# A layer with a long convolution, cross attention and a quantized feed-forward part: context and weights laid out on the host, context products from SBUF

## Chip, cores and metric

The kernel runs on one core of a Trainium2 chip. The metric is the device time of one execution in microseconds, lower is better. Engines are named as in the profile: PE is TensorE, PEld its weight loads, DVE is VectorE, ACT is ScalarE, POOL is GpSimd, and SP is the queue of SyncE, which issues all the DMAs.

## What is computed

A decoder layer with three parts, each with a residual and a layer norm: a Hyena convolution, a cross attention that is a convolution too, and a feed-forward part with weights rounded to -1, 0 and 1.

```python
x = _layernorm(x + hyena(x, ...))                       # (16, 256, 512)
# cross attention, k = v = ctx_2048, q = x, heads of 8 rows
kv = jnp.einsum('bhil,bhjl->bijhl', k_, v_)             # products of the context with itself
y = irfft(rfft(kv, 2 * L) * rfft(ssm_kernel, 2 * L))[..., :L]
out = jnp.einsum('bijhl,bhil->bjhl', y + kv * D, q_)
x = _layernorm(x + out)
# feed-forward: w1 (2048, 512), w2 (512, 2048)
w_quant = clip(round(w * rms), -1, 1) / rms
x_quant = clip(round(x * scale), -128, 127) / scale
h = gelu(x_quant @ w1_quant.T); out = quantized(h) @ w2_quant.T
x = _layernorm(x + out)
```

There are 32 heads of 8 rows, and 16 x 512 positions. As k and v are the same context, only 36 products of pairs are made for each position instead of 64.

## The kernel before

The program has two blocks. `hyena_block` does the first part for two halves of the batch and, toward its end, gets the rounded weights of the feed-forward part ready. `heads_block` then does cross attention and feed-forward head by head: one head is 16 x 8 = 128 rows of 512.

**The end of the first block.** In its last stretch the output projection is done in 16 blocks (`out_part` on TensorE, L554; `res_stat` and `res_norm` on VectorE). The residual has four buffers: SP loads block R + 3 when the result of block R - 1 has been stored (`load_res`, `store_res`). Between the blocks the eight parts of w1 and w2 are rounded: SP loads a part of 1 MB (`load_part`), ScalarE scales and rounds it (`round_part`), VectorE clips it (`clip_part`), TensorE turns 16 squares of 128x128 through PSUM (`turn_part`, L608), and ScalarE writes them as f16 from PSUM, half a part at a time (`copy_part`, L768). The context of the first head is turned here as well (`turn_first_ctx`), and its products are made after block 12 (`first_pairs`).

**The loop over heads.** Every engine has a `body(n)` with its instructions in a fixed order; step n works on several heads at once. For a head the context goes this way: SP loads 128 rows of 512 (`load_ctx`, 256 KB), ScalarE reverses each block of 128 (`reverse_blocks`, L1166), TensorE turns the four blocks into `ctx_bank` in PSUM (`turn_ctx`, L1395), ScalarE copies them to SBUF with each group of 8 written twice (`copy_twice` into `kx`, L1171), and VectorE makes the 36 products (`far_pairs`, L1183, 4 of them; `near_pairs`, L1177, 32 of them) with one operand from `ctx_bank` and the other from `kx`. `sum_blocks` (L1674) adds two blocks of products into `kv_sum`, both operands in SBUF.

The products then go through TensorE as a Toeplitz matrix product (L1412) into `conv_bank`, in four blocks `tb`. VectorE multiplies each with the query (`times_q_up`, `times_q_dn`, writing `z`), reading `conv_bank` in PSUM and `qx` in SBUF. GpSimd sums `z` in `add_up`, four instructions (L1830, L1832, L1835, L1839), the last of which writes `att`. `z` has two buffers, so VectorE's block `tb` waits for the `att` of block `tb` - 2. `att` is turned (`turn_back`), added to the residual and normalized, rounded, and goes through the feed-forward part one to four steps later.

The orders that matter are, on GpSimd in step n: `add_up` of the last block of head n-1; `rstd_of_out`, which waits for `o_mv`; `add_up` block 0 of head n; `rstd_of_att`; `add_up` blocks 1 and 2. On VectorE: last half of `z` of head n-1, scale of g, `z` block 0 (it waits for the `att` of block 2 of head n-1), `far_pairs` and `near_pairs` of head n+1, `o_mv` (`mean_of_out`), the output sum, the residual sum, `z` block 1, and so on, with `kv_sum` near the end.

Of the kernel before, what the change touches and what calls it, by code (L numbers as in the profile page):

```python
# [13 lines left out]
P = 128  # L14
# [4 lines left out]
F = 2048  # L19
# [33 lines left out]
def hyena_block(nc, w, early, dram):  # L53
# [24 lines left out]
    with ExitStack() as ctx:  # L78
# [130 lines left out]
        part_turned = sem("part_turned")  # L209
# [12 lines left out]
        PART_AT = {1 + i: i for i in range(2 * PARTS)}  # L222
        CTX_AT, PAIRS_AT = 11, 12
# [49 lines left out]
        with nc.Block() as block:  # L273
            @block.sync
            def _(sp):
# [50 lines left out]
                def part_source(i):  # L326
                    if i < PARTS:
                        return dram["w1"].rearrange("(q n p) d -> p q n d", p=P, q=PARTS)[:, i, :, :]
                    return dram["w2"][(i - PARTS) * P:(i - PARTS + 1) * P, :]

                def part_target(i, tile):
                    return tile.rearrange("p (n d) -> p n d", d=D) if i < PARTS else tile
# [82 lines left out]
                for hf in range(HALF):  # L415
                    if hf + 1 == HALF:
# [34 lines left out]
                    for t in range(T):  # L451
# [8 lines left out]
                        if hf + 1 == HALF and t == CTX_AT + 1:  # L460
                            sp.wait_ge(early["ctx_reversed"], 1)
                            sp.dma_start(early["ctx_tok"][:, 0, :], dram["ctx"][:, 2 * HD:3 * HD, :]).then_inc(early["ctx_loaded"][0], 16)

            @block.tensor
            def _(pe):
# [131 lines left out]
                def turn_part(i):  # L597
                    pe.wait_ge(clipped, i + 1)
                    low = view(part_raw[i].bitcast(F16), 0, (2, F))
                    for hh in range(2):  # L600
                        if i >= 2:
                            pe.wait_ge(part_done, 2 * (i - 2) + hh + 1)
                        elif hh == 0:
                            pe.wait_ge(ch_copied, 4 * HALF * DC)
                        out = turn_bank[2 * (i % 2) + hh][:, :, :].rearrange("p a b -> p (a b)").bitcast(F16)
                        for j in range(FC // 2):
                            fc = hh * FC // 2 + j
                            last = nc.tensor.transpose(out[:, j * P:(j + 1) * P], low[:, fc * P:(fc + 1) * P], w["ident16"][:, :])  # L608
                        last.then_inc(part_turned, 1)

# [577 lines left out]
def heads_block(nc, w, early, dram):  # L1188
# [6 lines left out]
    with ExitStack() as ctx:  # L1195
# [119 lines left out]
        with nc.Block() as block:  # L1315
            @block.sync
            def _(sp):
# [647 lines left out]
```

## Time and profile before

| | |
|---|---|
| median of three runs | 1036.88 us (1036.31 to 1039.31) |
| span of the profiled execution | 1030.8 us |
| busy: PE, PEld | 977.3 us (95%), 582.6 us (57%) |
| busy: DVE, ACT, POOL | 813.1, 617.1, 569.0 us (79%, 60%, 55%) |
| moved by DMA | 148.89 MB |

A busy share is an average over the whole span. GpSimd's 55% is made of a first half in which it has little to do and a second half in which it is busy nine tenths of the time, so the two halves are to be read apart. The first block ends near 457 us. The profiled execution's own time isn't given; its span is 6.1 us below the median.

### The profile page before, as it was taken

What the parts mean: (1) busy time and instruction counts of PE and PEld (TensorE: products, weight loads), DVE (VectorE), ACT (ScalarE), POOL (GpSimd) and SP (SyncE); (2) the same over time, 40 slices, a digit from 0 to 9 for tenths busy, and PEclk for the clock granted to TensorE, in tenths of its full rate; (3) what the DMA queues carried; (4) which work ended last, traced back from release to release, by engine and by line L of the source; (5) the groups of instructions that cost most, each with busy time, mean ns of one, the idle gap of its engine ahead of it and who ended that gap; (6) DMA issues with size and microseconds to landing.
All of it is one profiled execution on the core that took longest, in us unless ns stands there. A gap on an engine that the chain in (4) does not pass through costs nothing.

```text
span 1030.8 us, 14820 instructions
## 1 busy us (share of the span) xinstructions
PE 977.3 (95%) x4555; PEld 582.6 (57%) x4555; DVE 813.1 (79%) x1539; ACT 617.1 (60%) x759; POOL 569.0 (55%) x890
## 2 busy tenths in 40 slices
PE   3899999999999999988999999999999999999985
PEld 2455555544455554546666666666666666666641
DVE  6977985786554656666999898989889898989872
ACT  5755544202565657413676767777777777777674
POOL 5410410132000002439989888989898989898861
PEclk9999999999999999989999999999999999999997
DMA  9323655365576679453454646464646464544333
GB/s 320 77 62 123 183 169 168 117 197 172 165 251 208 204 245 310 146 166 86 86 129 106 144 105 146 103 148 99 150 101 149 103 141 110 134 114 111 77 73 81
DMA packets 186924, 148.89 MB, mean 144 GB/s; under 512 B 100501, under 2 KB 141497, under 8 KB 184825
## 3 DMA queue, kind: packets, MB, share of 16 engines
q1 hardware_dynamic: 186872, 148.26, 53.2%
q8 instruction: 26, 0.43, 0.2%
q14 instruction: 26, 0.20, 0.1%
HBM read 93.49 MB, written 33.77 MB: 123 GB/s over the span
## 4 chain that ended last, share of the span: by engine, by line
POOL 36%; DVE 7%; issue 5%; PE 5%; ACT 1%; POOLq 1%; DMA 0%; DVEq 0%; ACTq 0%
POOL sum L1830 15%; POOL sum L1832 8%; POOL att L1839 4%; POOL sum L1835 3%; PE conv_bank L1412 3%; DVE kv L1177 2%; POOL a_rstd L1849 1%; DVE block_diag L1177 1%; POOL o_rstd L1860 1%; DVE z L1700 1%; PE hq_bank L1481 1%; PE back_bank L1500 1%; POOL a_shift L1851 1%; POOL a_rstd L1846 1%; POOL o_shift L1862 1%
## 5 line engine op out<-in xcount | busy, mean ns | idle before, releaser
L1830 POOL TENSOR_TENSOR sum<-z 128x640 f32<-128x640 f32 x128 | 204.9, 1601 | 3.1 <-DVE z L1703 3.1
L845 DVE SCALAR_TENSOR_TENSOR conv_all<-u,taps,conv_all 128x1024 f32<-128x1024 f32 x92 | 122.4, 1331 | 91.3 <-ACT conv_all L716 89.4
L1412 PE MATMUL conv_bank<-block_diag 128*128 128x288 f32 x508 | 140.0, 416 | 3.6 <-ACT conv_bank L1569 1.9
L1412 PE MATMUL conv_bank<-kv,block_diag 128*128 128x288 f32 x512 | 137.5, 407 | 2.6 <-ACT conv_bank L1569 1.5
L1481 PE MATMUL hq_bank<-x_lo,hq_t 128*128 128x512 f16 x512 | 123.2, 386 | 4.0 <-DMA hq_t<-hq_int 4.0
L1691 DVE TENSOR_TENSOR z<-conv_bank,qx 128x512 f32<-128x512 f32 x128 | 88.0, 687 | 43.4 <-POOL att L1839 29.7
L708 ACT ACTIVATE u<-slot_bank,bias,unscale 128x1024 f32<-128x1024 f32 x46 | 55.4, 1205 | 108.5 <-PE slot_bank L517 82.5
L1832 POOL TENSOR_TENSOR sum<-sum 128x320 f32<-128x320 f32 x128 | 112.4, 878 | 10.0
L1412 PEld LDWEIGHTS conv_bank<-block_diag 128*128 128x128 f32 x508 | 96.7, 196 | 31.0 <-ACT conv_bank L1569 2.4
L554 PE MATMUL slot_bank<-wout_t,y 128*128 128x512 f32 x256 | 112.8, 594 | 0.0
L1412 PEld LDWEIGHTS conv_bank<-kv,block_diag 128*128 128x128 f32 x512 | 94.1, 190 | 29.3 <-DVE z L1703 2.6
L517 PE MATMUL slot_bank<-x_lo,w_hi 128*128 128x512 f16 x384 | 91.1, 379 | 3.3 <-DVE x_lo L833 3.3
L1055 POOL TENSOR_SCALAR r_rstd<-r_meanvar 128x1 f32<-128x1 f32 x32 | 19.7, 615 | 133.3 <-DVE r_meanvar L869 133.3
L517 PE MATMUL slot_bank<-x_hi,w_hi 128*128 128x512 f16 x384 | 91.1, 379 | 1.7 <-ACT x_hi L688 0.8
L517 PE MATMUL slot_bank<-x_hi,w_lo 128*128 128x512 f16 x384 | 91.0, 379 | 0.0
L1754 DVE TENSOR_REDUCE g_max<-g 128x1 f32<-128x512 f32 x128 | 86.3, 676 | 5.2 <-ACT g L1617 5.2
L1481 PEld LDWEIGHTS hq_bank<-x_lo,hq_t 128*128 128x128 f16 x512 | 50.7, 99 | 64.6 <-DMA hq_t<-hq_int 4.5
L554 PEld LDWEIGHTS slot_bank<-wout_t,y 128*128 128x128 f32 x256 | 47.6, 190 | 54.3 <-issue 53.8
L1617 ACT ACTIVATE g<-back_bank,x_unscale 128x512 f32<-128x512 f32 x64 | 43.8, 684 | 57.6 <-PE back_bank L1500 57.6
L1578 ACT ACTIVATE hq_f<-g,h_scale 128x1024 f32<-128x1024 f32 x64 | 73.5, 1148 | 5.8 <-DVE h_scale L1749 5.8
L1839 POOL TENSOR_TENSOR att<-sum 128x128 f32<-128x128 f32 x128 | 65.2, 510 | 10.4 <-POOL sum L1835 0.8
L1700 DVE TENSOR_TENSOR z<-conv_bank,qx 128x384 f32<-128x384 f32 x128 | 69.3, 541 | 0.0
(187 smaller groups left out, 1775.8 us busy)
## 6 DMA issues: line engine op xcount, KB each, us to landing
x_quad<-in_w SPq DMA_DIRECT2D x10, 1024.0 KB, 8.0
v_scratch<-conv_all SPq DMA_DIRECT2D x16, 512.0 KB, 3.3
c_scratch<-v_tok SPq DMA_DIRECT2D x8, 1024.0 KB, 5.3
y<-c_scratch SPq DMA_DIRECT2D x8, 1024.0 KB, 4.9
res<-in_x SPq DMA_DIRECT2D x32, 256.0 KB, 3.0
x_scratch<-res SPq DMA_DIRECT2D x32, 256.0 KB, 3.2
block_diag<-in_ctx SPq DMA_DIRECT2D x32, 256.0 KB, 5.0
block_diag<-ssm_scratch SPq DMA_DIRECT2D x32, 256.0 KB, 4.0
```

The costliest lines, as they stand in the source:

```text
L517: last = nc.tensor.matmul(slot_bank[n % 2][:, q, :], wt[:, dc, e * P:(e + 1) * P], xt[:, dc, cols], start=(j == 0 and dc == 0), stop=(j == ...
L554: last = nc.tensor.matmul(slot_bank[R // 2 % 2][:, R % 2, :], y[:, cc, t, :], w["wout_t"][:, cc, :], start=(cc == 0), stop=(cc == DC - 1))
L845: ins = nc.vector.scalar_tensor_tensor(out=acc, in0=(u_first[kind] if n < 3 else u)[:, t0 + tap:t0 + tap + T // 2, :].rearrange("p t b -> ...
L1412: last = nc.tensor.matmul(view(conv_bank[tb % 2][:, hh, :], 0, (ROW64, T // 2), (1, PAIRS)), toep[:, head.buf, window * P:(window + 1) * P ...
L1481: last = nc.tensor.matmul(hq_bank[:, :], hq_t[:, fc, :], w["w2_t"][:, fc, :], start=(fc == 0), stop=(fc == FC - 1))
L1578: nc.scalar.activation(hq_f[:, half], g[:, half], ACT.Copy, scale=h_scale[:, 0:1], bias=LOW_HALF).then_inc(hq_rounded, 1)
L1691: nc.vector.tensor_tensor(view(z[:, b, :, :], 0, (4 * PLANE, T), (PLANE + 1, 4), (1, HD)), view(conv, 0, (ROW64, T), (HD, 4), (1, HD)), vi ...
L1700: nc.vector.tensor_tensor(view(z[:, b, :, :], DN, (4 * PLANE, T), (PLANE, 3), (1, HD)), view(conv, HD, (ROW64, T), (HD, 3), (1, HD)), view ...
L1754: nc.vector.tensor_reduce(g_max[:, k:k + 1], g[:, k * 512:(k + 1) * 512], AX_X, ALU.max, apply_absolute_value=True).then_inc(g_maxed, 1)
L1830: nc.gpsimd.tensor_tensor(sum2[:, :, :], z[:, b, :, 0:half], z[:, b, :, half:2 * half], ALU.add).then_inc(sum2_done, 1)
L1832: nc.gpsimd.tensor_tensor(sum1[:, :, :], sum2[:, :, 0:PLANE], sum2[:, :, PLANE:half], ALU.add).then_inc(sum1_done, 1)
L1839: nc.gpsimd.tensor_tensor(att[:, head.buf, tb, :].rearrange("p (t j) -> p t j", j=HD), sum1[:, :, DN:PLANE], sum1[:, :, 0:HD], ALU.add).th ...
```

## The change

- The host hands over the context already turned and reversed, with each group of 8 written twice (`ctx_turned`, 32 x 128 x 1024), and w1 and w2 transposed. `load_ctx`, `reverse_blocks`, `turn_ctx`, `copy_ctx` and `ctx_bank` go; `load_kx` loads 512 KB a head straight into `kx`, which has two buffers now.
- `near_pairs` and `far_pairs` read both operands from `kx`.
- `turn_part` and `copy_part` go; `narrow_part` writes a whole part as f16 from SBUF. `turn_first_ctx` goes, and `first_pairs` comes after block 9.
- The f16 identity isn't made. The initial loads of parts are w1 in rows of 2048 and w2 in four pieces of 512.

```diff
-        PART_AT = {1 + i: i for i in range(2 * PARTS)}
-        CTX_AT, PAIRS_AT = 11, 12
+        PAIRS_AT = 9
...
-                            sp.dma_start(early["ctx_tok"][:, h, :], dram["ctx"][:, heads, :]).then_inc(early["ctx_loaded"][h], 16)
+                            sp.dma_start(early["kx"][:, h, :], dram["ctx_turned"][h]).then_inc(early["kx_loaded"][h], 16)
...
+                def narrow_part(i):
+                    act.wait_ge(clipped, i + 1)
+                    if i == 0:
+                        act.wait_ge(slot_full, HALF * NSLOT)
+                    out = (x_hi, x_lo)[i // PARTS][:, i % PARTS, :]
+                    nc.scalar.activation(out, view(part_raw[i].bitcast(F16), 0, (2, F)), ACT.Copy, bias=-HALF_ONE).then_inc(part_done, 1)
...
-def near_pairs(nc, k, kx, kv):
+def near_pairs(nc, kx, kv):
 
     W2 = 2 * HD
-    return nc.vector.tensor_tensor(view(kv, 0, (PAIRS, LB * T), (HD, 4), (1, HD)), view(k, 0, (HD, LB * T), (0, 4), (1, HD)),
+    return nc.vector.tensor_tensor(view(kv, 0, (PAIRS, LB * T), (HD, 4), (1, HD)), view(kx, 0, (W2, LB * T), (0, 4), (1, HD)),
                                    view(kx, 0, (W2, LB * T), (1, 4), (1, HD)), ALU.mult)
...
-def far_pairs(nc, k, kx, kv):
-
-    return nc.vector.tensor_tensor(view(kv, 4 * HD, (PAIRS, LB * T), (1, 4)), view(k, 0, (HD, LB * T), (1, 4)),
+def far_pairs(nc, kx, kv):
+
+    return nc.vector.tensor_tensor(view(kv, 4 * HD, (PAIRS, LB * T), (1, 4)), view(kx, 0, (2 * HD, LB * T), (1, 4)),
                                    view(kx, 4, (2 * HD, LB * T), (1, 4)), ALU.mult)
...
+                def load_kx(head):
+                    sp.wait_ge(kv_done, head.back(2).count(1, 1))
+                    sp.dma_start(kx[:, head.buf, :], dram["ctx_turned"][head.c]).then_inc(kx_loaded[head.buf], 16)
...
                 def body(n):
                     h1, h3 = n.back(1), n.back(3)
-                    if n.c == 0:
-                        load_ctx(n.back(-3))
+                    if n.c >= 1 and n.back(-2).exists():
+                        load_kx(n.back(-2))
...
-                    if n.back(-4).exists():
-                        load_ctx(n.back(-4))
```

In the instruction order this shows at three places. First SP's queue in one step of the loop over heads, before (`in_ctx` is the context, `x_scratch` the first part's result, `ssm_scratch` the Toeplitz rows):

```order
L1354 DMA_TRANSPOSE xq_t<-xq_int 128x4x128 [waits xq_packed]
L1320 DMA block_diag<-x_scratch 128x1x512 [waits x1_turned]
L1320 DMA x_res<-x_scratch 128x1x512 [waits a_steps]
L1335 DMA block_diag<-ssm_scratch 128x512 [waits conv_full]
L1336 DMA block_diag<-ssm_scratch 128x2x128
L1320 DMA block_diag<-in_ctx 128x1x512 [waits ctx_reversed]
L1358 DMA_TRANSPOSE hq_t<-hq_int 128x8x128 [waits hq_packed] x2
```

And after:

```order
L1306 DMA_TRANSPOSE xq_t<-xq_int 128x4x128 [waits xq_packed]
L1277 DMA block_diag<-in_ctx_turned 128x1024 [waits kv_done]
L1273 DMA block_diag<-x_scratch 128x1x512 [waits x1_turned]
L1273 DMA x_res<-x_scratch 128x1x512 [waits a_steps]
L1287 DMA block_diag<-ssm_scratch 128x512 [waits conv_full]
L1288 DMA block_diag<-ssm_scratch 128x2x128
L1310 DMA_TRANSPOSE hq_t<-hq_int 128x8x128 [waits hq_packed] x2
```

The context's load moved from behind the other loads of the step to before them and is twice as large.

Second TensorE at the end of a step, before (`z_done` frees a bank of the convolution):

```order
L1412 MATMUL conv_bank<-block_diag 128x8x36 x6
L1407 MATMUL back_bank<-ident,block_diag 128x128 [waits g_done,x1_loaded1]
L1407 MATMUL back_bank<-ident,block_diag 128x128 x3
L1395 MATMUL ctx_bank<-ident,block_diag 128x128 [waits kv_done,ctx_reversed]
L1395 MATMUL ctx_bank<-ident,block_diag 128x128 x3
L1412 MATMUL conv_bank<-kv,block_diag 128x8x36 [waits z_done,kv_done,toep_loaded1]
```

And after:

```order
L1441 MATMUL back_bank<-x_hi,xq_t 128x512 [waits g_done]
L1441 MATMUL back_bank<-x_hi,xq_t 128x512 x3
L1353 MATMUL conv_bank<-block_diag 128x8x36 x6
L1348 MATMUL back_bank<-ident,block_diag 128x128 [waits g_done,x1_loaded1]
L1348 MATMUL back_bank<-ident,block_diag 128x128 x3
L1353 MATMUL conv_bank<-kv,block_diag 128x8x36 [waits z_done,kv_done,toep_loaded1]
```

The four transposes of the context are gone, and nothing else moved.

Third VectorE at the products in a step, before (`z` is the product with the query, `o_mv` the mean and variance of the output):

```order
L1691 TENSOR_TENSOR z<-conv_bank,qx 128x16x4x8 [waits att_done]
L1700 TENSOR_TENSOR z<-conv_bank,qx 128x16x3x8
L1703 TENSOR_TENSOR z<-conv_bank,qx 128x16x8
L1660 REGISTER_ALU
L1662 REGISTER_ALU [waits kx_done]
L1183 TENSOR_TENSOR block_diag<-ctx_bank,block_diag 128x64x4 [waits conv_full]
```

And after, with the large product and `o_mv`, which follow in both:

```order
L1611 TENSOR_TENSOR z<-conv_bank,qx 128x16x4x8 [waits att_done]
L1620 TENSOR_TENSOR z<-conv_bank,qx 128x16x3x8
L1623 TENSOR_TENSOR z<-conv_bank,qx 128x16x8
L1581 ISA
L1583 REGISTER_ALU [waits kx_loaded0]
L1138 TENSOR_TENSOR block_diag<-block_diag 128x64x4 [waits conv_full]
L1704 ISA
L1706 REGISTER_ALU [waits o_steps]
L1132 TENSOR_TENSOR block_diag<-block_diag 128x64x32 [waits o_shifted]
L1690 BN_AGGR o_mv<-o_stats 128x2
```

The place is the same; the operand from `ctx_bank` has become one from `block_diag`, the SBUF tile in which `kx` lies, and the wait is for the load instead of ScalarE's copy.

## Rows read from the trace of the kernel before

**Rows 1.** Timeline of GpSimd (POOL): start us, duration us, instruction [idle before it].

```profile
539.51 0.19 POOL L1857 TENSOR_TENSOR o_rstd<-o_mv,eps_col 128x1 f32<-128x1 f32 x1 [1.26 <-DVE o_mv L1770]
...
963.36 0.19 POOL L1857 TENSOR_TENSOR o_rstd<-o_mv,eps_col 128x1 f32<-128x1 f32 x1 [0.82 <-DVE o_mv L1770]
```

**Rows 2.** Waits between 500 and 1000 us: total, times, longest.

```profile
DVE z L1691 <- POOL att L1839: 26.9, 26, 1.3
...
POOL o_rstd L1857 <- DVE o_mv L1770: 21.6, 26, 1.3
```

**Rows 3.** Timeline of VectorE (DVE), one step of the loop over heads.

```profile
705.15 0.69 DVE L1691 TENSOR_TENSOR z<-conv_bank,qx 128x512 f32<-128x512 f32 x1 [1.22 <-POOL att L1839]
...
706.42 0.41 DVE L1183 TENSOR_TENSOR block_diag<-ctx_bank,block_diag 128x256 f32<-128x256 f32 x1
706.75 2.28 DVE L1177 TENSOR_TENSOR block_diag<-ctx_bank,block_diag 128x2048 f32<-128x2048 f32 x1
708.95 0.17 DVE L1770 BATCH_NORM_AGGREGATE o_mv<-o_stats 128x2 f32<-128x6 f32 x1
...
717.70 0.98 DVE L1674 TENSOR_TENSOR kv_sum<-block_diag 128x576 f32<-128x576 f32 x1
...
722.08 0.69 DVE L1691 TENSOR_TENSOR z<-conv_bank,qx 128x512 f32<-128x512 f32 x1 [0.90 <-POOL att L1839]
```

**Rows 4.** Timeline of GpSimd in the same step.

```profile
704.97 1.55 POOL L1830 TENSOR_TENSOR sum<-z 128x640 f32<-128x640 f32 x1
706.60 0.87 POOL L1832 TENSOR_TENSOR sum<-sum 128x320 f32<-128x320 f32 x1
...
707.92 0.45 POOL L1839 TENSOR_TENSOR att<-sum 128x128 f32<-128x128 f32 x1
709.20 0.19 POOL L1857 TENSOR_TENSOR o_rstd<-o_mv,eps_col 128x1 f32<-128x1 f32 x1 [0.82 <-DVE o_mv L1770]
...
718.02 2.07 POOL L1830 TENSOR_TENSOR sum<-z 128x640 f32<-128x640 f32 x1
```

**Rows 5.** Timeline of TensorE (PE): two turns of the context; an earlier idle time.

```profile
702.16 0.60 PE L1395 MATMUL ctx_bank<-ident,block_diag 128*128 128x128 f32 x4
702.60 1.14 PE L1412 MATMUL conv_bank<-kv,block_diag 128*128 128x288 f32 x4
...
719.11 0.60 PE L1395 MATMUL ctx_bank<-ident,block_diag 128*128 128x128 f32 x4
...
489.41 1.24 PE L1412 MATMUL conv_bank<-block_diag 128*128 128x288 f32 x4 [1.93 <-ACT conv_bank L1569]
```

**Rows 6.** Groups of ScalarE (ACT) instructions: count, busy us, mean ns, idle before.

```profile
L1171 ACT COPY block_diag<-ctx_bank 128x1024 f32<-128x1024 f32 x31 | 31.5, 1017 | 0.0
...
L1166 ACT COPY block_diag<-block_diag 128x512 f32<-128x512 f32 x32 | 19.5, 612 | 1.3 <-DMA block_diag<-in_ctx 1.3
```

**Rows 7.** Timelines of VectorE and GpSimd where `kv_sum` meets GpSimd's instructions.

```profile
513.96 2.09 DVE L1674 TENSOR_TENSOR kv_sum<-block_diag 128x576 f32<-128x576 f32 x1
...
515.52 1.27 POOL L1832 TENSOR_TENSOR sum<-sum 128x320 f32<-128x320 f32 x1
...
734.50 0.75 DVE L1674 TENSOR_TENSOR kv_sum<-kv 128x576 f32<-128x576 f32 x1
...
734.56 1.00 POOL L1839 TENSOR_TENSOR att<-sum 128x128 f32<-128x128 f32 x1
```

**Rows 8.** Timelines of TensorE and VectorE near the end of the first half.

```profile
421.12 1.06 PE L608 MATMUL conv_bank<-ident,u 128*128 128x128 f16 x16
...
431.18 0.69 DVE L865 TENSOR_TENSOR res<-slot_bank,res 128x512 f32<-128x512 f32 x1 [1.55 <-DMA res<-in_x]
```

**Rows 9.** Stretches: busy PE, PEld, DVE, ACT, POOL; granted clock, DMA share, GB/s.

```profile
400.00:410.00 10.00, 9.64 (x52) 4.83 (x50) 5.21 (x9) 10.00 (x9) 3.98 (x4) 1.00 1.05 312
490.00:495.00 5.00, 5.00 (x17) 3.52 (x16) 4.39 (x8) 1.35 (x2) 4.46 (x9) 0.66 0.17 52
1000.00:1005.00 5.00, 3.47 (x17) 1.41 (x16) 3.86 (x13) 4.44 (x6) 1.02 (x4) 1.00 0.12 26
```

More of the change, by code:

```diff
@@ L595, in sum_matrix @@
                     nc.tensor.matmul(turn_bank[0][:, 0, 0:2], ones[:, :], total[:, :], start=True, stop=True).then_inc(summed, 1)
[L597 to L609, printed above, removed]
-                def turn_first_ctx():
-                    pe.wait_ge(early["ctx_reversed"], 1)
-                    pe.wait_ge(part_done, 2 * (2 * PARTS - 2) + 1)
-                    for lb in range(LB):
-                        last = nc.tensor.transpose(turn_bank[0][:, lb, :], early["ctx_rev"][:, 0, lb * P:(lb + 1) * P], w["ident"][:, :])
-                    last.then_inc(early["ctx_turned"], 1)
                 def convolve_first(tb):
@@ L1320, in load @@
                     return lambda: sp.dma_start(tile[:, head.buf, :], src).then_inc(loaded[head.buf], 16)
-                def load_ctx(head):
-                    start = load("ctx", ctx_tok, head, ctx_loaded)
-                    sp.wait_ge(ctx_reversed, head.back(2).count(1, 1))
-                    start()
+                def load_kx(head):
+                    sp.wait_ge(kv_done, head.back(2).count(1, 1))
+                    sp.dma_start(kx[:, head.buf, :], dram["ctx_turned"][head.c]).then_inc(kx_loaded[head.buf], 16)
                 def load_x1(head):
@@ L1388, in _ @@
             def _(pe):
-                def turn_ctx(head):
-                    pe.wait_ge(ctx_reversed, head.count(1, 1))
-                    if head.c >= 1:
-                        pe.wait_ge(kv_done, head.back(1).count(1, 1))
-                    for lb in range(LB):
-                        last = nc.tensor.transpose(ctx_bank[:, lb * P:(lb + 1) * P], ctx_rev[:, head.buf, lb * P:(lb + 1) * P], w["ident"][:, :])
-                    last.then_inc(ctx_turned, 1)
                 def turn_x1(head):
@@ L1935, with laid_out @@
 _INPUTS = {
-    "x": "x", "ctx_2048": "ctx", "L0_attn_ln_gamma": "ln_gamma", "L0_attn_ln_beta": "ln_beta", "L0_attn_W_in": "W_in",
+    "x": "x", "L0_attn_ln_gamma": "ln_gamma", "L0_attn_ln_beta": "ln_beta", "L0_attn_W_in": "W_in",
     "L0_attn_b_in": "b_in", "L0_attn_short_w": "short_w", "L0_attn_short_b": "short_b", "L0_attn_k": "k",
     "L0_attn_conv_bias": "conv_bias", "L0_attn_W_out": "W_out", "L0_xattn_ssm_kernel": "ssm_kernel",
-    "L0_xattn_D": "ssm_D", "L0_ffn_w1": "w1", "L0_ffn_w2": "w2",
+    "L0_xattn_D": "ssm_D",
 }
+def laid_out(inputs, np):
+    once = np.asarray(inputs["ctx_2048"]).reshape(T, H, HD, LB, P)[..., ::-1].transpose(1, 4, 3, 0, 2)
+    twice = np.stack([once, once], axis=4)
+    return {
+        "ctx_turned": np.ascontiguousarray(twice).reshape(H, P, LB * T * 2 * HD),
+        "w1_t": np.ascontiguousarray(np.asarray(inputs["L0_ffn_w1"]).T),
+        "w2_t": np.ascontiguousarray(np.asarray(inputs["L0_ffn_w2"]).T),
+    }
 def kernel(**inputs):
@@ L1955 @@
         dram[short] = nc.dram_tensor(f"in_{short}", a.shape, _mybir.dt.from_np(a.dtype), kind="ExternalInput").ap()
+    for short, a in laid_out(inputs, _np).items():
+        arrays[f"in_{short}"] = a
+        dram[short] = nc.dram_tensor(f"in_{short}", a.shape, _mybir.dt.from_np(a.dtype), kind="ExternalInput").ap()
     dram["out"] = nc.dram_tensor("out_0", (T, B, D), F32, kind="ExternalOutput").ap()
```

91 lines of the change are left out of this document (21 added, 70 removed).

## The prediction, made before the changed kernel ran

> **What bounds the kernel now.** I read the waits first, then the timelines of three engines over one step of the loop over heads, because that loop fills the second half of the run. Its steps are alike: GpSimd's first instruction of the output variance starts 26 times, at 539.51 first and at 963.36 last, so 25 steps take 16.95 us each [rows 1]. Over the same stretch VectorE waits 26 times for GpSimd's `att`, and GpSimd 26 times for VectorE's `o_mv` [rows 2]: the two wait for each other, once a step each.
>
> The ring can be followed in one step. VectorE starts `z` at 705.15, when GpSimd has finished an `att`; then come the small and the large product of the context (706.42 and 706.75) and `o_mv` at 708.95 [rows 3]. GpSimd meanwhile does one `add_up` from 704.97 on, is done before `o_mv` is there, idles 0.82 us, and starts the rest of its step at 709.20 [rows 4]. From there to the next `z` at 722.08 [rows 3] are 12.88 us of GpSimd work without a pause. So the ring is 4.05 us (705.15 to 709.20) plus 12.88 us, 16.93 us in all, and it has no slack except those 0.82 us, on GpSimd's side of its first part.
>
> TensorE is as full: from one transpose of the context to the next, 702.16 to 719.11, are 16.95 us, and its groups follow each other with no idle time [rows 5]. Two rings of equal length lie side by side. A saving on one of them alone is worth nothing, and a cost on one is paid at once.
>
> **What the change takes away in the loop.** TensorE loses four transposes a head, 702.16 to 702.60 or 0.44 us [rows 5]: its ring would be 16.51 us. ScalarE loses the copy with both halves (1017 ns) and the reversal (612 ns) [rows 6]; ScalarE is on neither ring, so this I cost at nothing, the cover being GpSimd's work. If TensorE alone set the pace, 31 heads would give 31 x 0.44 = 13.6 us. Since the other ring stands at 16.93 us, the gain is nothing: what is late next is `att`, as now.
>
> **What it adds in the loop.** The products have the same shapes, 128x256 and 128x2048, but both operands now come from SBUF. The trace has one such VectorE instruction in the loop, `kv_sum`, 576 elements. It and GpSimd's instructions exclude each other. At 717.70 it takes 0.98 us, against 0.75 us when it finds the way free [rows 3, 7], and GpSimd's `sum` at 718.02 takes 2.07 us [rows 4], against 1.55 us at 704.97: GpSimd lost 0.52 us. At 734.50 it is first and takes 0.75 us, and GpSimd's `att` beside it takes 1.00 us, where another takes 0.45 (707.92) [rows 4, 7]: lost 0.55 us. At 513.96 it comes just after a long GpSimd instruction has begun, takes 2.09 us, and the next GpSimd instruction takes 1.27 us [rows 7] where 0.87 is usual (706.60) [rows 4]: lost 0.40 us, and VectorE lost 1.34. The products with one operand from PSUM do no such thing: the large one runs from 706.75 to 709.03 across GpSimd's instruction at 706.60, which keeps its 0.87 us.
>
> So I price the lock at 0.52 us for 576 elements, 0.90 ns an element: 2304 elements make 2.08 us. The engine's own pace is higher: from 256 elements to 2048 the instruction grows from 0.41 to 2.28 us [rows 3], 1.04 ns an element, or 2.40 us for both; that is the cost with none of GpSimd's gaps between instructions used up. The upper end is both instructions whole, 0.41 + 2.28 = 2.69 us; the lower one is the 0.40 us collision, 1.60 us. I take 2.3, nearer to the pace of the large instruction, since it is long beside the gaps.
>
> The Trainium skill, "SBUF — State Buffer", section "Who interferes with whom", says that a VectorE instruction with two SBUF inputs and a GpSimd instruction that reads SBUF exclude each other for the whole instruction, and which issues first goes on. It speaks against this change; the trace agrees on the exclusion, while `kv_sum`, 0.75 us long, cost GpSimd only 0.52. With whole instructions (2.69 us) a step would be 0.39 us longer than I forecast, some 10 us in all.
>
> **The step after.** The products are issued 1.3 to 1.6 us after `att`, when GpSimd is inside the first instruction of `add_up` (704.97 to 706.52). VectorE waits about 0.1 us for it, then GpSimd stands still. Whether GpSimd gets a turn between the small and the large product changes only what comes first: its `add_up` of 3.40 us becomes 3.40 + 2.30 = 5.70 us. It ends at 704.97 + 5.70 = 710.67 instead of idling until 709.20. `o_mv` comes by 709.9 at the latest (large product started after the instruction of 0.87 us), so it no longer matters. The ring grows by 710.67 - 709.20 = 1.47 us to 18.4 us. Then GpSimd is never idle; TensorE, at 16.5 us of work, waits some 1.9 us a step, most likely before the transposes of `att`, and VectorE keeps its wait for `att`.
>
> **Sum for the loop.** 26 steps with a full ring at 1.47 us are 38.2 us. The five steps before have the products too but GpSimd idles more there, some 4 us in small waits, the largest but one being the 1.26 us before 539.51 [rows 1]. Five times 2.3 us is 11.5 us, less the 3.5 us of idle time that I take to be used up: 8 us. The last steps, after 963, have no products and stay. Together 46 us.
>
> **The first half.** The eight rounds of TensorE transposes of the weights go, about 1 us each (16 transposes, 1.06 us) [rows 8]; ScalarE writes the narrowed weights straight from SBUF in eight instructions instead of sixteen. In this stretch VectorE waits for the residual's DMA before each block (1.55 us at 431.18) [rows 8], because a load waits for the store of four blocks before; TensorE's share is hidden behind that, so I cost all of it at nothing. If that cover were not there, it would be worth 8 x 1.06, some 8.5 us. The first products move from block 12 to block 9, where the same 1.5 us waits absorb their 2.6 us as they do now. GpSimd has only two tiny instructions a block there. The f16 identity (one GpSimd cast at the start) goes; nobody waited for it, zero.
>
> The DMA grows: a head's context comes as 512 KB instead of 256 KB. Two of these loads lie in the queue before the stores of the first blocks, at 400 us, where the DMA engines are full at 312 GB/s [rows 9]. 2 x 256 KB at that rate are 1.7 us, and the chain of loads and stores starts that much later: +1.5 us, between 0 and 3. In the loop the load comes first in the step instead of fifth; it waits for products of a step ago, and behind it stand loads used a step later, so it costs nothing.
>
> **The number.** Span 1030.8 us, and 6.1 us around it to the median of 1036.9 us (the profiled execution's own total isn't given; the three runs lie within 3 us). 1036.9 + 46 + 1.5 = 1084.4; I say 1085.
>
> **The rivals.**
> A, a longer ring, 1095 to 1118. Two things lead there. `kv_sum` can come late, into a long GpSimd instruction, as at 513.96, where VectorE loses 1.34 us; if this repeats, VectorE's last `z` of the step is late and the step is up to 0.9 us longer: 26 x 0.9 = 23 us, 1108. Or TensorE's new pause costs it its clock: after an idle of 1.93 us the stretch from 490 to 495 us has a granted clock of 0.66, part of it at 1.2 instead of 2.4 GHz [rows 5, 9], 1.7 us lost. That speaks for 18.2 us on TensorE, still within 18.4; after idle times of 1.5 us near 1004 the clock stayed at 1.00 [rows 9]. Chance 0.2.
> B, a milder lock, 1050 to 1075. If GpSimd runs during part of the products, or the phases shift so that they meet its idle time, the cost is 0.5 to 1.2 us a step: 26 x 0.5 to 1.2 and half the ramp, 1036.9 + 17 to 37. The case of 0.40 us for 576 elements (1.60 in all) gives +0.78 a step, 1062. Chance 0.1.
> C, no exclusion for these instructions: the ring stays at 16.93 us and nothing is gained, 1036 to 1039. `kv_sum` speaks against it in all the cases shown. Chance 0.04.
> D, faster. TensorE is the bound, VectorE and GpSimd merely follow it, and there is no lock. It decides as soon as `att` is ready whenever TensorE is: 13.6 us in the loop and 8.5 us in the first half go, 1015. For it is TensorE without idle time; against it are the 26 waits for `att` and the collisions. Chance 0.04.
>
> **How the numbers follow.** The forecast, 1076 to 1094, has 0.62; A 0.2, B 0.1, C 0.04, D 0.04. The range, 1068 to 1108, takes in the forecast, the upper part of B and most of A; a lock of 1.85 us (1.0 us a step) gives its lower end, whole instructions plus a late `kv_sum` in half of the steps its upper. A run of this kernel can tell 0.3% (3 us) from no change. Faster 0.04, the same 0.04, slower 0.92.
>
> **What would show it.** In the profile after: GpSimd's `sum` beside the products at 3 to 4 us instead of 0.87 or 1.55, about 2.3 us a step more busy time on it; its wait for `o_mv` gone; the products at 2.2 to 3.2 us by where GpSimd stood; steps of 18.4 us; TensorE idle near 1.9 us a step; the first half within 3 us of before. GpSimd's instructions at their old lengths would sink the forecast, and so would steps of 16.5 us.

## The result and the profile after

The changed kernel takes 1071.55 us (median of 4 runs, 1069.96 to 1075.82) against 1036.6 us for the kernel before in the same session (1032.24 to 1039.31). The ratio is 1.0348, with a 95% interval of 1.0318 to 1.0378 (the brackets behind the ratios below are such intervals too): slower by some 35 us. The profiled execution of after has a span of 1073.8 us and a time of 1075.82 us.

The loop over heads is where the time went. GpSimd's timeline gives its period, with the same instruction as in [rows 1]: `o_rstd` of the first head in the steady part, and the one 25 steps later. Columns here and in the timelines below: start us, duration us, instruction, [idle before it].

```profile
556.64 0.19 POOL L1777 TENSOR_TENSOR o_rstd<-o_mv,eps_col 128x1 f32<-128x1 f32 x1
...
1005.99 0.19 POOL L1777 TENSOR_TENSOR o_rstd<-o_mv,eps_col 128x1 f32<-128x1 f32 x1
```

That is 449.35 us for 25 steps, 17.97 us each, against 16.95. The idle time before `o_rstd`, 1.26 and 0.82 us in [rows 1], has gone. GpSimd in one step, the stretch that answers to [rows 4]:

```profile
713.07 1.55 POOL L1750 TENSOR_TENSOR sum<-z 128x640 f32<-128x640 f32 x1
714.70 0.96 POOL L1752 TENSOR_TENSOR sum<-sum 128x320 f32<-128x320 f32 x1
715.74 2.22 POOL L1755 TENSOR_TENSOR sum<-sum 128x48 f32<-128x48 f32 x1
718.04 0.46 POOL L1759 TENSOR_TENSOR att<-sum 128x128 f32<-128x128 f32 x1
718.45 0.19 POOL L1777 TENSOR_TENSOR o_rstd<-o_mv,eps_col 128x1 f32<-128x1 f32 x1
...
721.13 0.87 POOL L1752 TENSOR_TENSOR sum<-sum 128x320 f32<-128x320 f32 x1
722.08 0.30 POOL L1755 TENSOR_TENSOR sum<-sum 128x48 f32<-128x48 f32 x1
722.45 0.45 POOL L1759 TENSOR_TENSOR att<-sum 128x128 f32<-128x128 f32 x1
...
726.87 0.84 POOL L1759 TENSOR_TENSOR att<-sum 128x128 f32<-128x128 f32 x1
```

And VectorE in the same step (compare [rows 3]):

```profile
713.25 0.69 DVE L1611 TENSOR_TENSOR z<-conv_bank,qx 128x512 f32<-128x512 f32 x1 [1.31 <-POOL att L1759]
...
714.52 0.41 DVE L1138 TENSOR_TENSOR kv<-block_diag 128x256 f32<-128x256 f32 x1
714.85 2.95 DVE L1132 TENSOR_TENSOR kv<-block_diag 128x2048 f32<-128x2048 f32 x1
717.73 0.17 DVE L1690 BATCH_NORM_AGGREGATE o_mv<-o_stats 128x2 f32<-128x6 f32 x1
...
726.56 0.85 DVE L1594 TENSOR_TENSOR kv_sum<-kv 128x576 f32<-128x576 f32 x1
...
731.21 0.69 DVE L1611 TENSOR_TENSOR z<-conv_bank,qx 128x512 f32<-128x512 f32 x1 [1.29 <-POOL att L1759]
```

Read the two together. The small product runs from 714.52 to 714.93, and GpSimd's L1752, which comes up at 714.70, takes 0.96 us instead of the 0.87 it takes at 721.13. The large product's record starts at 714.85, but it takes 2.95 us instead of 2.28: L1752, which runs until 715.66, has the turn, and the product comes after it and takes until 717.80. GpSimd's L1755 comes up at 715.74 and lasts until 717.96: 2.22 us for an instruction that takes 0.30 us at 722.08. So the pair costs GpSimd 0.09 + 1.92 = 2.01 us. `o_mv` is done at 717.9, and GpSimd comes to `o_rstd` only at 718.45, without a pause. By form, over 500 to 1000 us, the instruction of 48 elements is the one that grew (after, then before; columns: count, busy us, mean ns, idle before):

```profile
L1755 POOL TENSOR_TENSOR sum<-sum 128x48 f32<-128x48 f32 x112 | 85.3, 762 | 8.8
```

```profile
L1835 POOL TENSOR_TENSOR sum<-sum 128x48 f32<-128x48 f32 x118 | 35.1, 298 | 9.2
```

TensorE, which had no idle time in [rows 5], now waits once a step for `att` to turn. The timeline of TensorE, then the waits of 500 to 1000 us (total, times, longest):

```profile
716.09 1.13 PE L1353 MATMUL conv_bank<-block_diag 128*128 128x288 f32 x4
718.55 0.66 PE L1413 MATMUL back_bank<-ident,att 128*128 128x128 f32 x4 [1.32 <-POOL att L1759]
```

```profile
PE back_bank L1413 <- POOL att L1759: 34.0, 28, 1.9
DVE z L1611 <- POOL att L1759: 33.8, 31, 1.4
```

Two stretches, with the granted clock behind the five busy times (PE, PEld, DVE, ACT, POOL), answer to [rows 9]:

```profile
490.00:495.00 5.00, 5.00 (x17) 3.76 (x16) 3.69 (x11) 1.81 (x3) 4.60 (x9) 0.74 0.01 2
500.00:980.00 480.00, 446.08 (x2011) 284.75 (x2012) 427.48 (x875) 297.87 (x372) 448.78 (x632) 0.99 0.52 129
```

The end of the first half is marked by GpSimd's clearing of `z`, after and before:

```profile
464.98 2.27 POOL L1785 MEMSET z<- 128x1280 f32 x2 [1.33 <-POOLq L271]
```

```profile
457.23 2.27 POOL L1865 MEMSET z<- 128x1280 f32 x2 [1.33 <-POOLq L273]
```

With these marks the 43.0 us between the two spans (1073.8 and 1030.8) split into:

| stretch | before | after | difference |
|---|---|---|---|
| start to clearing of `z` | 457.23 | 464.98 | +7.75 |
| to the first `o_rstd` | 82.28 | 91.66 | +9.38 |
| 25 steps | 423.85 | 449.35 | +25.50 |
| to the end | 67.44 | 67.81 | +0.37 |

The medians differ by 34.95 us, which is the last three lines (35.3 us) without the first.

### The profile page after: what moved, and what is told of

The parts are those of the page before. It is cut to its first block, busy times and chain, and to the rows that moved or that the text cites. A ratio compares the mean times of both kernels' runs of the same rounds, so it can differ in the third digit from the quotient of the medians.

```text
span 1073.8 us, 14094 instructions
## 1 busy us (share of the span) xinstructions
PE 972.7 (91%) x4299; PEld 561.5 (52%) x4299; DVE 833.3 (78%) x1539; ACT 578.3 (54%) x687; POOL 626.2 (58%) x889
## 4 chain that ended last, share of the span: by engine, by line
POOL 47%; issue 4%; PE 3%; DVE 1%; ACT 1%; POOLq 1%; DMA 1%; ACTq 0%
POOL sum L1750 18%; POOL sum L1752 11%; POOL sum L1755 9%; POOL att L1759 5%; POOL a_rstd L1769 1%; POOL o_rstd L1780 1%; PE conv_bank L1353 1%; PE back_bank L1441 1%; PE hq_bank L1422 1%; POOL a_shift L1771 1%; POOL a_rstd L1766 0%; POOL o_shift L1782 0%; POOL o_rstd L1777 0%; POOL a_shift L1767 0%; POOL o_shift L1778 0%
## 5 line engine op out<-in xcount | busy, mean ns | idle before, releaser
L1750 POOL TENSOR_TENSOR sum<-z 128x640 f32<-128x640 f32 x128 | 199.1, 1556 | 3.0 <-DVE z L1623 3.0
L1353 PE MATMUL conv_bank<-kv,block_diag 128*128 128x288 f32 x512 | 140.8, 415 | 3.1 <-ACT conv_bank L1496 3.1
L1752 POOL TENSOR_TENSOR sum<-sum 128x320 f32<-128x320 f32 x128 | 116.5, 910 | 10.0
L1353 PEld LDWEIGHTS conv_bank<-kv,block_diag 128*128 128x128 f32 x512 | 96.5, 195 | 30.5 <-ACT conv_bank L1496 4.1
L1755 POOL TENSOR_TENSOR sum<-sum 128x48 f32<-128x48 f32 x128 | 93.9, 734 | 10.0
L515 PE MATMUL slot_bank<-x_hi,w_hi 128*128 128x512 f16 x384 | 93.5, 387 | 4.8 <-ACT conv_all L689 3.2
L1759 POOL TENSOR_TENSOR att<-sum 128x128 f32<-128x128 f32 x128 | 70.7, 552 | 10.4 <-POOL sum L1755 0.8
```

The source lines that it names most:

```text
L515: last = nc.tensor.matmul(slot_bank[n % 2][:, q, :], wt[:, dc, e * P:(e + 1) * P], xt[:, dc, cols], start=(j == 0 and dc == 0), stop=(j == ...
L1353: last = nc.tensor.matmul(view(conv_bank[tb % 2][:, hh, :], 0, (ROW64, T // 2), (1, PAIRS)), toep[:, head.buf, window * P:(window + 1) * P ...
L1750: nc.gpsimd.tensor_tensor(sum2[:, :, :], z[:, b, :, 0:half], z[:, b, :, half:2 * half], ALU.add).then_inc(sum2_done, 1)
L1752: nc.gpsimd.tensor_tensor(sum1[:, :, :], sum2[:, :, 0:PLANE], sum2[:, :, PLANE:half], ALU.add).then_inc(sum1_done, 1)
L1755: nc.gpsimd.tensor_tensor(sum1[:, :, DN:DN + 3], sum1[:, :, DN:DN + 3], sum1[:, :, HD:HD + 3], ALU.add).then_inc(sum1_more, 1)
L1759: nc.gpsimd.tensor_tensor(att[:, head.buf, tb, :].rearrange("p (t j) -> p t j", j=HD), sum1[:, :, DN:PLANE], sum1[:, :, 0:HD], ALU.add).th ...
```

## The experiments

Two theories at first. *Lock*: the products read both operands from SBUF and stop GpSimd, whose path is lengthened by what it loses less its idle time. *Load*: the context's load of 512 KB, earlier in SP's queue, delays what follows. Ratios below are to the kernel before, in runs on the same chip.

**One operand back to PSUM.** Everything of the change stays (host layout, load, no transposes, no reversal); ScalarE copies half of `kx` into a PSUM bank, and the products of the loop read one operand there (those of the first head, made in the first block, still read SBUF alone).

```diff
+                def copy_ctx(head):
+                    act.wait_ge(kx_loaded[head.buf], head.loads())
+                    act.wait_ge(kv_done, head.back(1).count(1, 1))
+                    nc.scalar.copy(ctx_bank[:, :].rearrange("p (n i) -> p n i", i=HD),
+                                   view(kx[:, head.buf, :], 0, (2 * HD, LB * T), (1, HD))).then_inc(kx_done, 1)
...
-                    near_pairs(nc, kx[:, head.buf, :], kv[head.buf]).then_inc(kv_done, 1)
+                    near_pairs(nc, ctx_bank[:, :], HD, kx[:, head.buf, :], kv[head.buf]).then_inc(kv_done, 1)
```

> The changed kernel, but ScalarE copies one half of each head's context from SBUF to a PSUM bank, and the products read one operand there again; loads, TensorE's order and the first half stay as changed. Lock theory (the products with two SBUF operands keep GpSimd out): GpSimd's instructions return to their usual lengths, its wait of 0.82 us for o_mv comes back, the step is 16.9 us as before, total within 3 us of before, ratio 0.997 to 1.004. Rival, the context's load of 512 KB at the head of SP's queue costs the time: the load is still there, the step stays near 17.97 us, ratio 1.033. Rival, TensorE alone sets the pace: step 16.5 us, ratio 0.987.

Measured: 1032.83 us, ratio 0.9977 (0.9958 to 0.9995), steps of 16.86 us. VectorE's large product and GpSimd beside it, and GpSimd's wait for `o_mv`:

```profile
707.41 2.28 DVE L1132 TENSOR_TENSOR block_diag<-ctx_bank,block_diag 128x2048 f32<-128x2048 f32 x1
```

```profile
708.21 0.29 POOL L1766 TENSOR_TENSOR sum<-sum 128x48 f32<-128x48 f32 x1
```

```profile
POOL o_rstd L1788 <- DVE o_mv L1701: 21.7, 26, 1.3
```

The instruction of 48 elements takes 0.29 us again under the large product, and the 26 waits for `o_mv` of [rows 2] are back. The loads of 512 KB are all there and cost nothing. The 35 us hang on where one operand of two instructions lies. Of the 0.44 us a step that TensorE saves, 0.09 come through at most; the ring of [rows 2] keeps the rest. The 0.09 may not be TensorE's at all: `kv_sum` meets GpSimd at another phase here and costs it 0.42 us a step on average instead of 0.52, read from 25 steps of each trace.

**The changed kernel once more**, beside three variants of it.

> The changed kernel once more, beside the experiments of this group. Theory: step 17.97 us, ratio 1.030 to 1.037; the first half ends 464.98 us in its first profile and 459.9 to 461.9 us in e1 and e3, which share this half word for word, so here it should end near 460 us and the span be some 4 us shorter than 1073.8 us. If the changed kernel delays its own first half, it ends at 465 us again.

Measured: 1069.29 us, 1.0321 (1.0298 to 1.0344), steps of 17.96 us. The clearing of `z` comes at 460.94 us in this profile, and the span is 1069.8 us: so the same code can differ by 4 us in this mark from one execution to the next.

**The large product in two instructions** of 1024 elements, to see whether GpSimd gets a turn between them.

```diff
-    return nc.vector.tensor_tensor(view(kv, 0, (PAIRS, LB * T), (HD, 4), (1, HD)), view(kx, 0, (W2, LB * T), (0, 4), (1, HD)),
-                                   view(kx, 0, (W2, LB * T), (1, 4), (1, HD)), ALU.mult)
+    W2, half = 2 * HD, LB * T // 2
+    for i in range(2):
+        last = nc.vector.tensor_tensor(view(kv, i * half * PAIRS, (PAIRS, half), (HD, 4), (1, HD)), view(kx, i * half * W2, (W2, half), (0, 4), (1, HD)),
+                                       view(kx, i * half * W2, (W2, half), (1, 4), (1, HD)), ALU.mult)
+    return last
```

> The changed kernel with the large product in two instructions of 1024 elements instead of one of 2048. Theory of the pace less a fixed part: each instruction keeps GpSimd out for its elements at 0.96 per ns less about 0.2 us that GpSimd's gap between instructions absorbs, so 2 x (1.07 - 0.2) = 1.73 us instead of the 1.92 us measured, and the step falls by 0.2 us to 17.8 us, ratio 1.028. Rival, the lock lasts as long as the whole instruction, start-up included: two instructions cost 0.15 us more, step 18.1 us, ratio 1.037. VectorE waits twice for GpSimd now; if that made VectorE the bound, the step would pass 18.2 us.

Measured: 1064.91 us, 1.0286 (1.0261 to 1.0311), steps of 17.75 us. GpSimd in a step:

```profile
708.20 1.16 POOL L1757 TENSOR_TENSOR sum<-sum 128x48 f32<-128x48 f32 x1
709.44 1.31 POOL L1761 TENSOR_TENSOR att<-sum 128x128 f32<-128x128 f32 x1
```

Two instructions lose 0.86 us each, 1.72 us instead of 1.92. GpSimd does get its turn between two VectorE instructions that follow each other directly, and each of these stops costs it some 0.2 us less than VectorE's work in it: at the pace of [rows 3], 1.04 ns an element, 1024 elements are 1.07 us and 2048 are 2.13.

**The large product twice**, the first time into a buffer that nobody reads.

```diff
+                    near_pairs(nc, kx[:, head.buf, :], kv_again)
                     near_pairs(nc, kx[:, head.buf, :], kv[head.buf]).then_inc(kv_done, 1)
```

> The changed kernel with the large product made twice, the first time into a tile that nobody reads (extra work, same output). Lock theory: GpSimd stands still 1.9 to 2.1 us more per head, step 17.97 + 2.0 = 20.0 us, total 31 x 2.0 = 62 us over the changed kernel, ratio 1.092 to 1.098. Rival, the cost sits in VectorE's own time: VectorE had about 1.3 us of idle time a step, so 2.2 us more would add 0.9 us a step, ratio 1.06.

Measured: 1139.44 us, 1.0994 (1.0967 to 1.1022), 70 us above the changed kernel.

```profile
704.42 2.23 POOL L1757 TENSOR_TENSOR sum<-sum 128x48 f32<-128x48 f32 x1
706.72 2.38 POOL L1761 TENSOR_TENSOR att<-sum 128x128 f32<-128x128 f32 x1
```

The second stop costs 1.93 us as the first does. The product is doubled for 31 heads, 31 x 1.93 = 60 us, and 10 us more were not foreseen. Some 5 of them are seen in the trace. In 17 of 25 steps `kv_sum` takes 0.75 to 0.87 us and the step 19.8 to 20.0 us, 17.97 + 1.93 and a little. In the other eight it meets a long instruction of GpSimd and takes 2.0 us, and the step is 20.4 to 20.7; in six of these GpSimd idles again, 2.6 us or more. That is what rival A's first mechanism, a late `kv_sum`, would look like. What the rest is, I have not separated; the clock's mean over the span is 0.956, against 0.975 in the changed kernel.

**Only the weights turned by the host**, in the kernel before.

```diff
-                def turn_part(i):
...
-                def copy_part(i):
...
+                def narrow_part(i):
```

> The kernel before, with w1 and w2 alone turned by the host: no weight transposes on TensorE in the last blocks of the first half, ScalarE narrows from SBUF; the context goes its old way. Theory, that stretch is bound by the chain of loads and stores of the residual: within 3 us of before, ratio 0.997 to 1.003, end of the first half within 2 us. Rival, TensorE bounds it: 8 x 1.06 = 8.5 us less, ratio 0.992. Rival, the narrowing or the new load pattern delays the first half by the 7.8 us by which the changed kernel's profile ends it later: ratio 1.007.

Measured: 1035.25 us, 1.0001 (0.998 to 1.0021). The 8.5 us of TensorE transposes are worth nothing there.

**`o_mv` ahead of the products, in the kernel before.** `o_mv` is what GpSimd waits for in [rows 2].

```diff
                         times_q_dn(n, 0)
+                    if n.back(5).exists() and n.exists():
+                        mean_of_out(n.back(5))
                     if n.back(-1).exists():
                         products_first(n.back(-1))
...
+                    if n.back(-1).exists():
+                        products(n.back(-1))
+                    if n.back(5).exists() and not n.exists():
...
-                    if n.back(-1).exists():
-                        products(n.back(-1))
-                    if n.back(5).exists():
                         mean_of_out(n.back(5))
```

> The kernel before, with o_mv made ahead of the two products instead of behind them, so that GpSimd needn't wait 0.82 us for it. Theory of two rings of equal length: TensorE's own 16.95 us of work a step remains, step 16.95 us, ratio 0.997 to 1.003. Rival, the ring of VectorE and GpSimd alone is the bound: step 16.93 - 0.82 = 16.1 us, 26 x 0.85 = 22 us less, ratio 0.979.

Measured: 1034.55 us, 0.9994 (0.9981 to 1.0007). GpSimd no longer waits for `o_mv` (it waits for `a_mv` and `z` instead, 0.7 to 1.4 us a step), and the step stays at 16.95 us on average, which is TensorE's length in [rows 5]. With one of two rings of equal length loosened, the other one holds. That it is TensorE's, the next run supports: with the same order on VectorE and GpSimd, but without the four transposes, the step does fall.

**Both: the operand from PSUM and `o_mv` early.** TensorE's ring is then shorter by its four transposes, and GpSimd's by its wait.

> e1 and e2 together: one operand in PSUM, no context transposes on TensorE, o_mv ahead of the products. Two rings: GpSimd's ring falls to 16.1 us and TensorE's to 16.5 us, so the step is 16.5 us, 26 x 0.43 = 11 us less than before, ratio 0.987 to 0.991. If TensorE was no bound, e2 falls already; if the other ring holds for a reason besides o_mv, this one stays at 16.9 us, ratio 1.000.

Measured: 1029.55 us, 0.9948 (0.9929 to 0.9967), the only version faster than the kernel before by more than 0.3%. The steps take 16.73 us on average: four of 25 are 16.43 to 16.51 us, TensorE's forecast length, and most of the others are 16.74 to 16.77. `kv_sum` meets GpSimd like this in all of them:

```profile
735.47 1.56 POOL L1766 TENSOR_TENSOR sum<-z 128x640 f32<-128x640 f32 x1
```

```profile
735.66 1.98 DVE L1605 TENSOR_TENSOR kv_sum<-kv 128x576 f32<-128x576 f32 x1
```

GpSimd began 0.19 us earlier, and VectorE stands still for 1.23 us of the 1.98. The lock works in both directions, and VectorE is busy for 464 of 480 us in this version. I took this for what keeps the others at 16.76; but `kv_sum` takes 1.96 to 1.98 us in the steps of 16.43 us too, so it isn't what tells the two kinds apart, and their difference stays unexplained.

**`kv_sum` elsewhere.** So I moved `kv_sum` to where GpSimd does two short instructions.

```diff
                         attend(h1)
                         dve.wait_ge(a_steps, h1.count(3, 2))
+                    if n.back(-1).exists():
+                        sum_blocks(n.back(-1))
...
-                    if n.back(-1).exists():
-                        sum_blocks(n.back(-1))
```

> e3_psum_mv_early with kv_sum moved: it now stands behind the statistics of the residual sum and before z of block 1, where GpSimd is in its two short instructions of 0.30 and 0.45 us, instead of after the maximum of g, where it always waited for the end of GpSimd's instruction of 1.55 us. Theory: in e3_psum_mv_early VectorE had no idle time in most of a step of 16.76 us, because kv_sum took 1.98 us instead of 0.75, and so VectorE held TensorE (16.5 us of work) back. With kv_sum at 0.75 to 1.1 us the step is TensorE's, 16.50 to 16.60, the ratio to the kernel before 0.987 to 0.993. Rival one: the z of block 1, which now comes 0.6 us later, holds TensorE back in its turn (its bank comes free later), the step stays 16.7 to 16.9 and the ratio 0.993 to 0.998. Rival two: 16.76 us is set by GpSimd, whose work is then unchanged, ratio 0.994 to 0.996 and kv_sum short all the same.

Measured: 1037.01 us, 1.0025 (1.0007 to 1.0044), steps of 17.0 us. The theory is wrong, and rival one, the only one of the three that allowed for a loss by the new place, set it too low and at TensorE. `kv_sum` is short now, and GpSimd waits longer (the last line is of the waits from 500 to 980 us):

```profile
735.72 0.76 DVE L1605 TENSOR_TENSOR kv_sum<-kv 128x576 f32<-128x576 f32 x1 [0.31 <-DVE a_stats L1648]
```

```profile
737.25 0.19 POOL L1782 TENSOR_TENSOR a_rstd<-a_mv,eps_col 128x1 f32<-128x1 f32 x1 [1.42 <-DVE a_mv L1651]
```

```profile
POOL a_rstd L1782 <- DVE a_mv L1651: 39.1, 27, 2.2
```

I had put the 0.76 us between the sum of the residual and `a_mv`. GpSimd waits there for `a_mv`, 1.4 us a step, and all its later sums are late by it. An instruction shortened by 1.2 us, put on the path of a wait, made the step 0.3 us longer (17.03 against 16.73 on average).

**`o_mv` early in the changed kernel.** If GpSimd alone is the bound, nothing waits for `o_mv` any more.

> The changed kernel with o_mv ahead of the products. Theory: with both operands in SBUF GpSimd has no idle time left, it is the bound by itself, and no longer waits for o_mv: moving o_mv is worth nothing, 17.9 to 18.0 us a step and a ratio of 1.030 to 1.034. Rival: the step still hangs on the order of the small instructions around the products (o_mv late after a long product), then 0.3 to 0.8 us a step come back and the ratio is 1.010 to 1.026.

Measured: 1070.18 us, 1.0346 (1.0325 to 1.0367), steps of 18.0 us, as with the changed kernel. The same edit is worth nothing here for another reason than in the kernel before: there TensorE held, here GpSimd is never idle.

**Less work for GpSimd.** The changed kernel without the instruction of 48 elements, which leaves GpSimd 0.37 us less work four times a step, so its sums are incomplete.

```diff
-                    nc.gpsimd.tensor_tensor(sum1[:, :, DN:DN + 3], sum1[:, :, DN:DN + 3], sum1[:, :, HD:HD + 3], ALU.add).then_inc(sum1_more, 1)
-                    pool.wait_ge(sum1_more, head.count(4, tb + 1))
```

> The changed kernel without GpSimd's third instruction in add_up (the sum of 48 elements is left out, four times a head, so some sums are incomplete). Theory, GpSimd is the bound after the change: 4 x 0.38 us = 1.5 us less a step, which would be 16.5 us, and TensorE's own work of 16.5 us comes next; step 16.5 to 16.7 us, ratio 0.990 to 0.997. Rival, VectorE or TensorE is the bound since the change: step stays near 17.97 us.

Measured: 1047.4 us, 1.0116 (1.0092 to 1.0141), steps of 16.6 to 17.7 us. GpSimd was the bound, for 22 us came back; but not down to TensorE's 16.5 us a step. The steps are of two kinds. In 10 of 25 `kv_sum` takes 0.75 us, GpSimd has next to no idle time, and the step is 16.6 to 16.8 us, near the 16.5 to 16.7 expected. In 15 `kv_sum` takes 1.97 to 2.10 us, and the step is 17.4 to 17.7; GpSimd idles 3 us in 14 of them, most of it before `o_mv`. One of these steps, VectorE and then GpSimd:

```profile
706.30 2.09 DVE L1594 TENSOR_TENSOR kv_sum<-kv 128x576 f32<-128x576 f32 x1
```

```profile
715.73 0.19 POOL L1775 TENSOR_TENSOR o_rstd<-o_mv,eps_col 128x1 f32<-128x1 f32 x1 [2.31 <-DVE o_mv L1690]
```

The two go together step by step; which causes the other is tried by two more runs, with the same instruction left out. First with `o_mv` early:

> e7_less_gpsimd (the changed kernel without GpSimd's third instruction of add_up on 48 elements, so its sums are incomplete) with o_mv ahead of the products. In e7_less_gpsimd GpSimd idled 2.3 us before o_mv and VectorE had hardly any idle time, kv_sum at 1.98 to 2.09 us, and the ratio was 1.012. If VectorE's own chain of work set the step there, o_mv early changes nothing: 1.009 to 1.014. If the wait for o_mv was part of the ring, as in the kernel before, it goes: the step falls to 16.6 to 16.9, ratio 0.992 to 1.002.

Measured: 1044.55 us, 1.0088 (1.0070 to 1.0106), steps of 17.28 us, `kv_sum` at 1.7 to 1.9 us. The wait for `o_mv` was not what held. VectorE is busy for 465.76 of 480 us:

```profile
500.00:980.00 480.00, 467.94 (x2105) 294.26 (x2104) 465.76 (x918) 312.01 (x387) 437.60 (x549) 1.00 0.53 134
```

Then with `kv_sum` moved as above too:

> e10_less_mv_early with kv_sum moved behind the statistics of the residual sum, as in e8_sum_early; GpSimd's third instruction is left out here too. If VectorE sets the step of e10_less_mv_early by waiting inside kv_sum for a long GpSimd instruction, this gives back 0.5 to 1.0 us a step, a ratio 0.012 to 0.025 below that of e10_less_mv_early. If GpSimd or TensorE sets it, the two ratios agree within 0.003.

Measured: 1045.62 us, 1.0103 (1.0085 to 1.0122), steps of 17.12 us; the two ratios agree within 0.003. `kv_sum` takes 0.76 to 1.15 us now. VectorE's busy time falls, and a wait takes its place:

```profile
500.00:980.00 480.00, 469.26 (x2120) 298.78 (x2119) 452.27 (x922) 313.44 (x390) 442.31 (x553) 1.00 0.55 134
```

```profile
POOL a_rstd L1769 <- DVE a_mv L1640: 14.6, 28, 1.4
```

The last line is again of the waits from 500 to 980 us. So below 17.3 us no single engine or wait can be named: TensorE, VectorE and GpSimd are all near full, and what is taken off one turns up as a wait at the next. Which of them sets 17.1 us stays open.

## Why the prediction was right, and where it was off

The range, 1068 to 1108, holds 1071.55. The mechanism is the forecast's: products from SBUF stop GpSimd, its idle time before `o_mv` is used up, it alone sets the step, TensorE waits before the transposes of `att`, and VectorE keeps its wait for `att`. The forecast's own interval, 1076 to 1094, doesn't hold it; the size is that of rival B, the milder lock, which had 0.1 and 1050 to 1075 (its sum, 1036.9 + 17 to 37, gives 1054 to 1074). The range holds the result because its lower end had been worked out from a lock of 1.85 us.

| term | forecast | measured |
|---|---|---|
| GpSimd's loss to the products, a step | 2.30 | 2.01 |
| idle time used up | 0.82 | 0.83 |
| `kv_sum` against GpSimd | no change | 0.12 less |
| longer step | +1.47 | +1.02 |
| 26 steps | +38.2 | +26.5 |
| the steps before | +8 | +8.4 |
| first half | +1.5 | 7.75 in one execution, about 0 in the medians |
| around the span | 6.1 | about 2 |

**The lock.** The term of 2.3 us was the one mis-sized. I had two prices: 0.90 ns an element from `kv_sum`'s collision in [rows 3, 4], 2.08 us in all, and VectorE's own pace, 1.04 ns, 2.40 us. I chose near the upper one, with the reason that the instruction is long beside the gaps. The runs show a smaller price where VectorE had to wait for a GpSimd instruction and the next GpSimd instruction waits for that one too, as within `add_up`: GpSimd loses VectorE's work at 1.04 ns an element, less about 0.2 us for each stop. For 2048 elements it is 1.92 of 2.13 us, for 1024 0.86 of 1.07, for 576 0.40 of 0.60, for 256 0.09 of 0.27. With two stops that is 2.40 - 0.4 = 2.0 us. Of these four tenths I had deducted one, with "GpSimd's gaps between instructions"; the other three are the larger part of the 0.45 us by which the longer step was overrated. The sign that I had named, a `sum` of 3 to 4 us, didn't come either: GpSimd got a turn between the two products, and the large one met the instruction of 48 elements, at 2.22 us.

The 0.2 us are no constant of the lock, and my own rows could have shown it. At 717.70 `kv_sum` waits for an `att`, takes 0.98 us, and the `sum` behind still loses 0.52 us [rows 3, 4]. That `sum` reads another buffer and follows the `att` without a gap. In the 12 steps of the kernel before in which `kv_sum` falls behind an `att`, GpSimd loses 0.51 to 0.53 us each time; behind the instruction of 48 elements in the changed kernel it loses 0.37 to 0.40. That the dependence between GpSimd's instructions makes the difference fits all these, but no run varied it alone.

**`kv_sum`.** It costs GpSimd 0.39 us now (`att` at 726.87, 0.84 instead of 0.45) instead of 0.52 [rows 4], because it now falls behind the instruction of 48 elements and no longer behind or just ahead of an `att`. Which collision occurs follows from the phase of the two engines, and I had taken the phase as given. 2.01 - 0.83 - 0.12 gives 1.06, against 1.02 measured.

**The ramp** came out near the forecast, 9.4 us with one full step of 1.02 in it.

**The first half** I put at +1.5, by the DMA. In the profiled executions the clearing of `z` comes at 457.23 and 459.34 with the first half of before in it, and between 457.81 and 464.98 in eleven executions with that of after (464.98 is the highest; mean 461.4). The difference of the means is 3 us, at the end of my 0 to 3, but single executions of the same code spread over 7 us, and the medians leave no room for it. It can't be called shown. That TensorE's transposes of the weights were hidden is shown: 1.0001 without them, and the clearing of `z` at 457.88. VectorE's wait for the residual's DMA, which I had before each block, comes 12 times for 16 blocks in the trace of before, 16.9 us in all.

**Around the span** I took the 6.1 us between one span and the median of other executions. The profiled executions with their own times have about 2 us around the span (1075.82 and 1073.8; 1071.9 and 1069.8). The span of before, 1030.8, so belongs to a time near 1032.8, some 4 us below the median, and the sum should have started from the median plainly. As it did so in effect, the predicted time isn't touched.

**TensorE's pause** is 1.27 us a step, where I had 1.9 for a step of 18.4; 17.97 - 16.5 is 1.47, and the rest is in small gaps.

**The rivals.** A needed `kv_sum` late or a lower clock. `kv_sum` takes 0.85 us in the steady part, and with a pause of TensorE in every step (34.0 us in 28 waits) the granted clock of the loop is 0.99. A late `kv_sum` does go with a longer step, though: in the runs with the product made twice and with less work for GpSimd, steps in which it takes 2 us are 0.5 to 1.0 us longer than the others; A's price was up to 0.9. C and D fall with GpSimd's 2.22 us. D's other claim, that the transposes would be worth 13.6 us if TensorE were the bound, is tested in part by the PSUM operand with `o_mv` early: four steps do take 16.43 to 16.51 us, the average is 16.73, and the whole is 1029.55 us.

**What the Trainium skill says**, in "SBUF — State Buffer", section "Who interferes with whom", held in its direction: such a VectorE instruction contends with a GpSimd instruction that reads SBUF, and the one that issued first goes on. By whole instructions it would have been 2.69 us a step; the trace shows 2.01.

## What to carry to other kernels

Before an operand of a VectorE instruction moves from PSUM to SBUF, look whether GpSimd runs beside it and how much idle time GpSimd has in that loop: the instruction becomes work for both engines, at VectorE's pace, less some 0.2 us a stop in the cases that pay least, and only the idle time pays for it. Work taken off TensorE and ScalarE is worth next to nothing while another ring of the same length stands beside them; here undoing the one costly part and loosening the second ring together gave 0.5% where each alone gave 0.2% or nothing. An instruction that collides may be moved, but first look which wait lies behind its new place. And before a step is called bound by one engine, look whether all its steps are alike: a mean of 17.2 us was made of steps of 16.6 and 17.6.

## What was new about the hardware

- GpSimd gets a turn between two VectorE instructions with both operands in SBUF that follow each other directly; it isn't starved. The large product of 2.28 us stood 0.67 us longer for that, 2.95 us.
- A stop within `add_up`, for which VectorE had waited, costs GpSimd about 0.2 us less than VectorE's work in it, for sizes from 256 to 2048 elements. Behind an `att`, whose successor doesn't wait for it, 576 elements cost 0.52 us instead of 0.40. Halving the large product saved 4.4 us of the whole time, in spite of one instruction more.
- The other direction is dearer: an instruction of 576 elements that came 0.19 us behind a GpSimd instruction of 1.56 us took 1.98 us instead of 0.75. Where this alternates with the short form from step to step, the steps differ by 0.5 to 1.0 us.
